# A bias split into three bf16 parts: in a 16x80 tile at the head, spread to its rows by DMA, in place of full-width GpSimd instructions

## The reference, cut to what matters

```python
def mx_linear(x, W, b):
    y = jnp.einsum('btk,ok->bto', mx_quant(x), mx_quant(W))
    return bf16_round(y + b)

h = mx_linear(h, W1, b1)     # 256 -> 1024
h = mx_gelu(h)
h = mx_linear(h, W2, b2)     # 1024 -> 256
```

## Time and profile before

| | before |
|---|---|
| median of 3 runs | 303.47 us (303.46 to 304.25) |
| the profiled execution's own time | 305.63 us |
| its span in the trace | 303.8 us |
| mean granted PE clock | 0.978 |

### The profile page before, as it was taken

The page is one execution under the profiler, slowest core; times in us unless marked ns, Lnnn a source line. Parts: engine busy times, 40 slices in busy tenths (PEclk is TensorE's granted clock), DMA queues, the critical chain, the costliest instruction groups (busy, mean ns, idle before and its releaser), DMA issues.

```text
span 303.8 us, 5403 instructions
## 1 busy us (share of the span) xinstructions
PE 276.3 (91%) x1696; PEld 167.9 (55%) x1696; DVE 273.4 (90%) x665; ACT 222.9 (73%) x364; POOL 186.1 (61%) x255
## 2 busy tenths in 40 slices
PE   7998897889798999999999999999699969999887
PEld 3675555557536664667466746674346344533543
DVE  3899999999989989998999899989995998889893
ACT  4130465485898889998999899899968997875551
POOL 2929568478565678767876787675755555422321
PEclk9999999999999999999999999999869996999999
DMA  7930020102003000102010201020000000000111
GB/s 234 364 106 1 0 85 22 35 10 63 1 2 104 0 2 0 37 2 76 31 36 2 94 10 37 1 72 1 9 0 2 35 1 2 35 0 2 37 36 37
DMA packets 10067, 12.30 MB, mean 40 GB/s; under 512 B 2995, under 2 KB 7347, under 8 KB 9782
## 3 DMA queue, kind: packets, MB, share of 16 engines
q1 hardware_dynamic: 9606, 11.16, 11.6%
q10 hardware_dynamic: 432, 0.79, 0.7%
HBM read 9.85 MB, written 2.10 MB: 39 GB/s over the span
## 4 chain that ended last, share of the span: by engine, by line
PE 52%; DVE 23%; ACT 14%; issue 5%; POOL 3%; DMA 2%; ACTq 0%; POOLq 0%; DVEq 0%
PE bank L2059 9%; PE bank L2034 8%; PE bank L2072 8%; DVE am L1351 4%; DVE nm L1265 4%; PE bank L1968 3%; PE bank L1994 3%; PE bank L2113 3%; PE bank L2138 3%; ACT p_sb L848 3%; DVE wam L1351 2%; ACT y_sb L862 2%; ACT L848 2%; ACT xT L841 2%; PE bank L2111 2%
## 5 line engine op out<-in xcount | busy, mean ns | idle before, releaser
L1265 DVE TENSOR_REDUCE nm<-bank 128x4 f32<-128x512 f32 x128 | 84.2, 678 | 8.2 <-PE bank L2034 7.0
L848 ACT ACTIVATE p_sb<-bank 128x512 f32<-128x512 f32 x128 | 71.9, 599 | 16.8 <-PE bank L2059 16.1
L2034 PE MATMUL bank<-kbd,xT 96*128 96x512 f32 x128 | 58.4, 473 | 5.7 <-DVE nm L1265 3.0
L2059 PE MATMUL bank<-xT,kbd 104*128 104x512 f32 x128 | 55.4, 457 | 5.2 <-ACT p_sb L848 3.3
L543 POOL TENSOR_TENSOR kbd<-k3r,diag_sb 96x512 fp32r<-96x512 f32 x32 | 32.9, 1039 | 15.2 <-PE bank L2059 15.2
L486 POOL TENSOR_SCALAR ve<-mv 128x2 f32<-128x2 f32 (+1 forms) x36 | 12.3, 342 | 42.6 <-DVE mv L1226 38.4
L2034 PEld LDWEIGHTS bank<-kbd,xT 96*128 96x128 f32 x128 | 24.5, 194 | 22.0 <-DVE nm L1265 12.2
L2059 PEld LDWEIGHTS bank<-xT,kbd 104*128 104x128 f32 x128 | 24.5, 197 | 20.5 <-ACT p_sb L848 11.6
L2072 PE MATMUL bank<-p_sb,va_sb 128*32 128x512 f32 x256 | 34.6, 631 | 0.1
L1351 DVE TENSOR_REDUCE am<-g_sb 128x32 f32<-128x1024 bf16 x16 | 30.3, 1894 | 0.9 <-ACT g_sb L868 0.9
L841 ACT ACTIVATE xT<-bank 8x1024 fp32r<-8x1024 bf16 x16 | 16.2, 1013 | 14.9 <-PE bank L2047 14.6
(11 more groups left out here) (124 smaller groups left out, 624.5 us busy)
## 6 DMA issues: line engine op xcount, KB each, us to landing
xt_sb<-in_xt SPq DMA_DIRECT2D x8, 256.0 KB, 3.1
x_sb<-in_x SPq DMA_DIRECT2D x8, 256.0 KB, 3.0
out_dram<-o_sb SPq DMA_DIRECT2D x7, 256.0 KB, 2.2
k_sb<-in_ctx SPq DMA_DIRECT2D x8, 192.0 KB, 2.6
x_all<-in_w SPq DMA_DIRECT2D x1, 1024.0 KB, 5.5
w_raw<-in_w SPq DMA_DIRECT2D x1, 1024.0 KB, 7.8
p_sb<-in_wkv ACTq DMA_DIRECT2D x2, 256.0 KB, 4.2
cv_sb<-in_ctxv SPq DMA_DIRECT2D x8, 64.0 KB, 2.0
```

The costliest lines, as they stand in the source:

```text
L848: sc.activation(p_sb[:, k, :], bankB[k % 2][:, :], ACT.Exp, scale=SCORE_SCALE).then_inc(s_ex, 1)
L1265: ve.tensor_reduce(nm[:, b, u, g, :], bankA[(2 + k + 11 * b) % 2][:, :].rearrange("p (k t) -> p k t", k=KU), AX.X, ALU.max, negate=True).t ...
L2034: mm(bankA[(2 + k + 11 * b) % 2][:, :], xT[0:MR, b, u, g, :], kbd[0:MR, b, u, :, :].rearrange("r k t -> r (k t)"), start=True, stop=True). ...
L2059: mm(bankB[k % 2][:, :], kbd[0:MR + 2 * KU, b, u, kk, :], xT[0:MR + 2 * KU, b, u, :, :].rearrange("r g s -> r (g s)"), start=True, stop=Tr ...
```

## The change

The bias is split in a small tile. SP loads the row as 16 partitions x 80 (one transfer in place of three, without a wait). GpSimd splits it there with four instructions, all directly behind `keys_rounded(0)`: high, rest, middle, low. `split_bias(1)`, `(2)` and `(3)` leave GpSimd's head, with the two 32-row moves; nothing else changes its place on GpSimd. A new step `spread_bias` stands in SP's queue between xt(1) and w1. It waits until the four instructions are done (`s_biasc` at 4) and starts three SBUF-to-SBUF transfers, which write the 1,280 numbers of each part into one row of `bias_h`. `bias_h` is zeroed in place of `bias_f`. The first `ffn_up` waits for the three transfers.

```diff
+        BR = 16
+        bias_f = sb("bias_f", [BR, (F + D) // BR], F32)
+        bias_rest = sb("bias_rest", [BR, (F + D) // BR], F32)
+        bias_parts = sb("bias_parts", [BR, 3, (F + D) // BR], BF16)
...
             def load_bias():
+                sp.dma_start(bias_f[:, :], bias.rearrange("o (r n) -> (o r) n", r=BR)).then_inc(s_w["bias"], 16)
+
+            def spread_bias():
                 sp.wait_ge(s_seta, 2)
+                sp.wait_ge(s_biasc, 4)
                 for n in range(3):
-                    sp.dma_start(bias_f[32 * n:32 * n + 1, :], bias).then_inc(s_w["bias"], 16)
+                    sp.dma_start(bias_h[32 * n:32 * n + 1, :], bias_parts[:, n, :]).then_inc(s_w["bias_rows"], 16)
...
                 load_xt(1)
+                spread_bias()
                 load_weight("w1")
                 load_weight("ln")
                 load_weight("w2")
...
-                gp.memset(bias_f[:, :], 0.0).then_inc(s_seta, 1)
+                gp.memset(bias_h[:, :].bitcast(F32), 0.0).then_inc(s_seta, 1)
...
+            def split_bias():
+                pool.wait_ge(s_w["bias"], 16)
                 hold(pool)
+                gp.tensor_scalar(bias_parts[:, 0, :], bias_f[:, :], 1.0, 0.0, ALU.mult, ALU.add).then_inc(s_biasc, 1)
+                pool.wait_ge(s_biasc, 1)
+                gp.tensor_tensor(bias_rest[:, :], bias_f[:, :], bias_parts[:, 0, :], ALU.subtract).then_inc(s_biasc, 1)
+                pool.wait_ge(s_biasc, 2)
+                hold(pool)
+                gp.tensor_scalar(bias_parts[:, 1, :], bias_rest[:, :], 1.0, 0.0, ALU.mult, ALU.add).then_inc(s_biasc, 1)
+                pool.wait_ge(s_biasc, 3)
+                gp.tensor_tensor(bias_parts[:, 2, :], bias_rest[:, :], bias_parts[:, 1, :], ALU.subtract).then_inc(s_biasc, 1)
...
                 keys_rounded(0)
-                split_bias(0)
+                split_bias()
...
                 rstd(0, ve1, rs1, s_ve1, s_rs1, 1)
-                split_bias(1)
                 split_xt_low(2)
...
                 shift(1 - 1, nb1, s_nb1)
-                split_bias(2)
                 split_x1_high(1, 0)
...
                 split_xt_low(3)
-                split_bias(3)
                 keys(1, 1, 0)
...
-                        pe.wait_ge(s_biasc, 6)
+                        pe.wait_ge(s_w["bias_rows"], 48)
```

More of the change, by code:

```diff
@@ L80, in decoder_kernel @@
         w2T = sb("w2T", [P, FC, D], BF16)
-        bias_f = sb("bias_f", [96, F + D], F32)
+        BR = 16
+        bias_f = sb("bias_f", [BR, (F + D) // BR], F32)
+        bias_rest = sb("bias_rest", [BR, (F + D) // BR], F32)
+        bias_parts = sb("bias_parts", [BR, 3, (F + D) // BR], BF16)
         bias_h = sb("bias_h", [96, F + D], BF16)
-        bias_rest = sb("bias_rest", [96, F + D], F32)
-        bias_mid = sb("bias_mid", [96, F + D], BF16)
-        bias_low = sb("bias_low", [96, F + D], BF16)
         ones_b = sb("ones_b", [96, P], BF16)
@@ L199, in ffn_bank @@
             return (bankP if b == 0 else bankA)[h]
-        s_w = {k: sem(f"loaded_{k}") for k in ("wkv0", "wkv1", "wq", "wo", "tri", "ident", "diag", "ln", "w1", "w2", "bias")}
+        s_w = {k: sem(f"loaded_{k}") for k in ("wkv0", "wkv1", "wq", "wo", "tri", "ident", "diag", "ln", "w1", "w2", "bias", "bias_rows")}
         s_x = sem("x_loaded")
@@ L440, in setup @@
                 gp.memset(va_heads[:, :, VH + DH:VH + DH + 1], 1.0).then_inc(s_seta, 1)
[L442 to L451, removed]
-                hold(pool)
[L453 to L469, removed]
+            def split_bias():
+                pool.wait_ge(s_w["bias"], 16)
+                hold(pool)
+                gp.tensor_scalar(bias_parts[:, 0, :], bias_f[:, :], 1.0, 0.0, ALU.mult, ALU.add).then_inc(s_biasc, 1)
[6 more added lines that the diff above has]
+                gp.tensor_tensor(bias_parts[:, 2, :], bias_rest[:, :], bias_parts[:, 1, :], ALU.subtract).then_inc(s_biasc, 1)
             def shift_product(p, mv, rs, nb, rs_ready, nb_ready):
@@ L515, in split_xt_low @@
                 if p == 2:
-                    pool.wait_ge(s_biasc, 2)
+                    pool.wait_ge(s_rs1, PB)
                 if p == 3:
```

## The result

The changed kernel takes 311.3 us (median of 4 runs, 308.15 to 313.29) against 303.47 us (4 runs), a ratio of 1.02 with a 95% interval of 1.0145 to 1.0255. The ratios leave out runs that lie over 1.5% above the fastest of their kernel (313.29 here); the medians have all runs in them. The prediction was 309.1 us, range 305.6 to 311.6. Measured again beside the kernel before, 6 runs gave 311.99 us against 305.0 us (29 runs), a ratio of 1.0235 [1.0176, 1.0293]. Single runs of either kernel differ by several us; those of before lie between 302.3 and 309.3.

A forecast was written before the change was run, and what follows sets the result against it. PE (busy 91%) and DVE (90%), handing work to each other in fixed order, were taken to bound the kernel. Late w1 5.3, clock 2.0 and freed low part -1.7 gave +5.6 us: 309.1 us, range 305.6 to 311.6.

The forecast's parts named there:

- w1 late: DVE's first read of w1 moves from 12.38 to 17.65 us: 5.3 us late (3.9 to 6.1).
- three issues of 0.30 us, as for the three bias loads: In SP's queue, three spreading transfers ahead of w1 take 0.30 us each; w1 goes out at 12.65.
- The keys did not land earlier: In the head, one bias issue replaces three, so the keys may land up to 0.6 us earlier.
- The later loads cost nothing: Behind w1 in SP's queue, w2 lands at about 20.9 us and costs nothing, or some tenths.
- The pause and the clock: PE pauses 5.1 us ahead of out_proj(0, 1) and its clock falls to 1.2 GHz: +2.0 us (0 to 4).
- some 5: Late in the trace of before, the clock's fall was read as some 5 us at half speed.
- 2.5 us lost, less 0.55: After PE's pause, 5 us of work at half speed loses 2.5 us, less 0.55 us idle ahead of 20.19.
- The rule of the Trainium skill: PE's default state is throttled and activity releases it; by that rule its pause costs 2.0 us, sum 309.1.
- the clock holds: Rival: PE's clock doesn't fall in the head; +3.6 us, 307.1 us, chance 0.27.
- The freed low part: At 49 us, without GpSimd's wide low part, DVE is free sooner: -1.7 us (0 to -2.45).
- The stalled product at 49.6 us: One DVE product of L1360 took 3.117 us, otherwise 0.66 to 0.68, said to end with the low part.
- The sum: Whole kernel: 5.3 + 2.0 - 1.7 = +5.6 us, median from 303.47 to 309.1 us.

The follow-up runs named there:

- experiment 1: Changed kernel with the three spreading transfers moved behind w2 in SP's queue; 304.36 us against 305.89 for before, ratio 0.9974.
- experiment 2: Kernel before, with SP issuing w1 only when the first wide bias instruction is done; 309.91 us against 305.89 for before.
- experiment 9: Changed kernel with one spreading transfer ahead of w1 and two behind w2; 309.52 us against 305.13 for before.
- experiment 3: Changed kernel with 26 warm matmuls in place of 2 ahead of out_proj(0, 1); 308.95 us against 305.89 for before.
- experiment 6: Kernel before, with GpSimd waiting for DVE's split maxima ahead of rounding xt(3); 304.13 us, ratio 0.9964 to before.
- the later traces of before: Kernel before, unchanged, profiled two more times; medians 305.43 us (12 runs) and 306.11 us (1 run).
- the second trace of before: Kernel before, unchanged, measured and profiled again; median 305.43 us in 12 runs.
- the first trace of before: Kernel before, unchanged, the original profile that the other traces are compared with; profiled execution 305.63 us.

## Why the prediction was right, step by step

- **w1 late: the mechanism right, the size 6.4 in place of 5.3 us.** The split ended at 11.78 (forecast 11.7) and the landing took 5.0 us (forecast 5.0). The step that was mis-sized is "three issues of 0.30 us, as for the three bias loads": they took 0.61 us each. I had priced a transfer from SBUF by rows of transfers from HBM. Experiments 1, 2 and 9 show that w1's place behind the wait and the issues, with the clock's fall that follows from it, is the loss, and nothing else in the change. The keys did not land earlier by anything that mattered: GpSimd began them at 7.82, and at 7.96 before.
- **The later loads cost nothing, as said.** w2 landed 7.1 us after its issue at 14.85, 21.95, and DVE read it at 22.97 without a wait.
- **The pause and the clock: right in kind, too dear.** The pause was 5.55 us (forecast 5.1), and the clock fell in every trace of the changed kernel. It cost 1.05 us in the profiled execution and 0.3 to 1.7 in others, not 2.0. The stretch of slow work was sized well, 4.6 us of about 5, though from a misread row: late in before the clock was down for 7 us (218.4 to 225.4), not "some 5". The mis-sized term is "2.5 us lost, less 0.55", which took PE's slow work as if it set the pace all the time. DVE was busy with block maxima meanwhile and waited only 0.99 us, for a copy of v; the clock was back by 26.5 as well. The rule of the Trainium skill that was weighed (TensorE: Matmul & The Clock Gate, "What's actually happening") came true, with 0.50 granted in the pause; the rival "the clock holds" is refuted, by experiment 3 as well, in which work in the pause keeps the clock up.
- **The freed low part: the number right, the reason half right.** 1.76 us came back, forecast 1.7. The stalled product at 49.6 us was a fact, and it went away (it ended at 52.7, half a us behind the low part, not with it). But the prediction took it as a steady cost of the low part. Experiments 2 and 6 and the later traces of before show 2.05 to 2.9 us regained with the low part in place: it hurt only in the trace in which xt(3) landed early enough for GpSimd to go ahead of DVE's splits of the maxima. The rows of that earlier collision (46.07, 0.62 us) were in the trace and I read past them, since only the largest stall was looked for.
- **The sum.** Forecast 5.3 + 2.0 - 1.7 = 5.6; in the pair of traces 6.4 + 1.05 - 1.76 = 5.7. The near hit is luck in part: the first term was 1.1 too low and the second 1.0 too high. The timed difference (7.8 and 7.0 us) is larger than the pair of traces gives: the profiled execution of before lay 2.16 us above its median, that of after at its median. That other executions of before have part of the freed time already would make it larger, and two traces show such executions; but they took 305.59 and 306.11 us in all, so this isn't shown to be the reason.
- **What stays open.** Between 212 and 267 us PE's clock falls twice in every trace, before and after, at times that differ by execution, and over this stretch the end moves by between -1.4 and +2.8 us against mark 2. Nothing was tried against it, so neither that the clock moves the end nor how much of the medians' difference lies there is shown.

## What to carry to other kernels

A wait put into a queue that works in order is paid by what stands behind it, not by what it guards: here a 70 us deadline was met by holding back a load that was needed within 0.2 us of landing. Before adding one, look for the first reader of each thing behind it, and put the new step behind the last urgent one. And price a stall between two engines only after asking what decides their meeting; where a single landing time does, a wait that fixes the order can be worth more than removing the work. At mark 2 it was here (2.75 against 1.85 us in single traces, experiments 6 and 1); the medians, 304.13 and 304.36, don't tell the two apart.

## What the runs showed of the hardware that was not expected

- Starting a transfer from SBUF to SBUF (16 x 160 bytes to one row) took SP 0.58 us in experiment 9, and w1, which took 0.33 before, took 0.57 directly behind it (0.58 behind three); in experiments 1 and 2, with no such transfer ahead, w1 took 0.33 again.
- A DVE split of 0.18 us that met a GpSimd instruction waited until that one ended: the split that began at 46.07 ended with GpSimd's 0.62 us rounding at 46.66, the next one at 47.7 with the keys at 47.65. This is the exclusive pair of ports of the Trainium skill (SBUF — State Buffer, "SBUF: two separate sides": for DVE instructions in a mode that takes two ports, or with two inputs in SBUF against a GpSimd one that reads SBUF, whichever starts first holds the pair for the whole instruction), and the traces agree. It works both ways: where DVE went first, GpSimd's keys took 1.54 us in place of 1.03. When the recorded starts are within 0.1 us, they don't tell who goes first: at 31.60 in the second trace of before DVE was recorded 0.06 us ahead and still waited, while in the first, 0.07 us ahead at the same place, it didn't. DVE's maxima of a PSUM tile (L1265) were not held up: 0.68 us at 53.26, beside a 32-row move of GpSimd.
- A difference of 0.7 to 1.0 us in one load's landing went with a shift of the whole rest of the kernel by about 1 us (mark 2 of experiments 1 and 4), and together with the low part by up to 2.9 (the first trace of before against experiment 2, between the marks).
